# A one-layer transformer kernel in float32: the end part moved into both branches, and its steps reordered

## The reference

```
for w in range(16):                       # for each head of 16
    s = (Q*cpm[w]) @ (K*cpm[w]).T * SCALE # 512x512 for each of 8 sequences
    acc += softmax(s*cos(KERR*s*s)) @ V * iw[w]
x1 = ln(x + (acc/16) @ Wo + bo)
h1, h2 = x1 @ sw1.T + sb1, x1 @ sw2.T + sb2
sh = ln(silu(h1)*h2) * s_ln_g + s_ln_b    # 64 wide
shared = sh @ sw3.T + sb3
xm = x1[rows]                             # 256 chosen rows
scores = sigmoid(xm @ eg_w.T + eg_b); e = argmax(scores + exp_bias)
w_s, w_e = softmax([sigmoid(xm @ sg_w.T + sg_b), scores[e]])
z = ln(silu(xm @ ew1[e].T + eb1[e]) * (xm @ ew2[e].T + eb2[e])) * sel_ln_g + sel_ln_b
shared[rows] = shared[rows]*w_s + (z @ ew3[e].T + eb3[e])*w_e
out = ln(x1 + shared)
```

## Time and profile before

| what | value |
|---|---|
| three runs | 3448.43, 3453.41, 3458.12 us (median 3453.41) |
| the profiled execution, its own time | 3451.96 us |
| its span | 3449.9 us |
| ACT busy | 3334.6 us (97%) |
| DVE busy | 3152.2 us (91%) |
| PE busy | 2711.8 us (79%) |

### The profile page before, as it was taken

The page is one execution under the profiler, slowest core; times in us unless marked ns, Lnnn a source line. Parts: engine busy times, 40 slices in busy tenths (PEclk is TensorE's granted clock), DMA queues, the critical chain, the costliest instruction groups (busy, mean ns, idle before and its releaser), DMA issues.

```text
span 3449.9 us, 47792 instructions
## 1 busy us (share of the span) xinstructions
PE 2711.8 (79%) x20599; PEld 778.2 (23%) x20599; DVE 3152.2 (91%) x2977; ACT 3334.6 (97%) x610; POOL 199.5 (6%) x325
## 2 busy tenths in 40 slices
PE   7887778887778887778887788887888887888763
PEld 2222222222222222222222222222222222222222
DVE  8899899899899899899899999999999999999977
ACT  7999999999999999999999999999999999999971
POOL 0000000000000000000010011110011110011111
PEclk8899999999999999999999999999999899999886
DMA  1000000000000000000000000000000000000010
GB/s 50 1 1 1 1 1 1 1 1 1 1 1 1 1 1 1 1 14 1 1 3 1 4 2 4 2 4 1 2 4 2 4 2 1 4 2 4 2 30 28
DMA packets 20759, 16.10 MB, mean 5 GB/s; under 512 B 4225, under 2 KB 18962, under 8 KB 20306
## 3 DMA queue, kind: packets, MB, share of 16 engines
q1 hardware_dynamic: 19282, 12.34, 1.2%
q10 hardware_dynamic: 1152, 0.53, 0.1%
q0 software_dynamic: 128, 0.26, 0.0%
HBM read 7.76 MB, written 5.37 MB: 4 GB/s over the span
## 4 chain that ended last, share of the span: by engine, by line
ACT 61%; issue 30%; ACTq 4%; DVE 3%; PE 2%; DMA 0%; SPq 0%; POOL 0%; DVEq 0%; POOLq 0%
ACT probs L656 56%; ACT probs L653 4%; ACTq L646 4%; PE psum L1273 1%; DVE m_pad L865 0%; ACTq L650 0%; DVE s_t L877 0%; ACT probs L680 0%; DVE probs L1190 0%; DVE probs L928 0%; DMA iw<-nterference_weights_dram 0%; SPq L468 0%; DVE x_p L743 0%; DVE x_p L735 0%; DVE x_p L739 0%
## 5 line engine op out<-in xcount | busy, mean ns | idle before, releaser
L656 ACT ACTIVATE probs<-s_t 128x8192 f32<-128x8192 f32 x447 | 3101.2, 7090 | 2.2 <-PE psum L1273 2.2
L1273 PE MATMUL psum<-probs,v_pad 128*27 128x512 f32 x15232 | 1992.5, 665 | 602.5 <-ACT probs L656 583.8
L1273 PEld LDWEIGHTS psum<-probs,v_pad 128*27 128x27 f32 x15232 | 485.3, 115 | 2036.1 <-issue 1095.5
L723 DVE SCALAR_TENSOR_TENSOR x_y<-s_t,c_last,x_2k 128x2048 f32<-128x2048 f32 (+1 forms) x160 | 344.1, 2150 | 2.3
L735 DVE SCALAR_TENSOR_TENSOR x_p<-x_p,x_y 128x2048 f32<-128x2048 f32 (+1 forms) x160 | 332.6, 2079 | 4.5
L743 DVE SCALAR_TENSOR_TENSOR x_p<-x_p,x_2k 128x2048 f32<-128x2048 f32 (+1 forms) x160 | 332.1, 2075 | 3.9
L731 DVE SCALAR_TENSOR_TENSOR x_p<-x_y 128x2048 f32<-128x2048 f32 (+1 forms) x160 | 330.9, 2068 | 3.3 <-PE psum L756 3.3
L739 DVE SCALAR_TENSOR_TENSOR x_p<-x_p 128x2048 f32<-128x2048 f32 (+1 forms) x160 | 331.5, 2072 | 2.4
L877 DVE COPY s_t<-psum 128x2048 f32<-128x2048 f32 x128 | 292.2, 2284 | 21.8 <-PE psum L839 21.1
L865 DVE TENSOR_REDUCE m_pad<-psum 128x4 f32<-128x2048 f32 x128 | 292.4, 2286 | 10.8 <-PE psum L802 9.7
L756 PE MATMUL psum<-x_p,v_pad 128*27 128x512 f32 x1152 | 174.5, 620 | 51.9 <-DVE x_p L743 51.4
(11 more groups left out here) (240 smaller groups left out, 1116.0 us busy)
## 6 DMA issues: line engine op xcount, KB each, us to landing
s_t<-in_L_attn_x_dram SPq DMA_DIRECT2D x4, 256.0 KB, 6.9
x_next_dram<-x_p SPq DMA_DIRECT2D x1, 1024.0 KB, 4.5
x_group<-x_next_dram SPq DMA_DIRECT2D x1, 1024.0 KB, 4.9
loop_memory<-in_L_attn_x_dram SPq DMA_DIRECT2D x8, 128.0 KB, 2.2
x_dram<-loop_memory SPq DMA_DIRECT2D x8, 128.0 KB, 1.8
out_dram<-loop_memory SPq DMA_DIRECT2D x8, 128.0 KB, 1.8
x_dram<-probs SPq DMA_DIRECT2D x2, 512.0 KB, 3.3
out_dram<-probs SPq DMA_DIRECT2D x2, 512.0 KB, 3.6
```

Of the source, the lines that this page charges most:

```text
L656: nc.scalar.activation(probs[:, (p + w) % 2, :], s_t[:, p, :], ACT.Exp, scale=scales[(p + w) % 2]).then_inc(s["exp_done"], 1)
L723: nc.vector.scalar_tensor_tensor(out=y, in0=scores, scalar=scale, in1=at, op0=ALU.mult, op1=ALU.subtract) \
L1273: last = nc.tensor.matmul(products_of(u, wg)[L * b:L * b + SLOTS * A, :], v_pad[:, p, b * T + kt, c0:c0 + SLOTS * A], probs[:, (p + w) % 2 ...
```

## The change

- **Both branches.** The end part of PE and DVE is called at the end of each branch (`tail_pe`, `tail_dve`), so no jump lies ahead of it; ACT, POOL and SP keep one copy behind the branches.
- **Prepared in unit 31.** DVE's memsets stand in step 5, the sum x+bo (before on POOL) in step 7, and the turning of the experts' weights (PE) and their copies (before on ACT) in step 8. SP's loop ends one chunk early and the last is written out, so that loads of x and of the experts' weights stand between its parts. The scratch memory is laid out so that what is prepared lies in the first buffer of `s_t`.
- **Chosen rows first.** Their turning, gates and products with all experts stand before stages 6 and 7 of the shared branch on PE; the two branches have norms of their own, and the sums and statistics of stage 7 are woven into the chosen rows' steps (`rest_piece`, `rest_out`). The stores and the scatter stay in their order.
- **Silu.** The biases sb1, sb2 are added by a product of one row (`one_row`) into the bank before stage 4, sigmoid replaces exp, 1+ and reciprocal, and DVE multiplies from PSUM chunk by chunk. The same for the gates. ACT loads the table for Sigmoid and later the one for Exp.
- **Gain and shift.** `sw3_t` is scaled by the norm's gain and `sb3` gets sw3 times its shift at the start of the kernel (`ln_col`), so the two instructions per chunk go.
- The masked experts are summed as a tree of halves, no longer by a reduction.

The core of the diff. At the start, ACT (first piece) and PE:

```diff
-            nc.scalar.activation(sw3_t[:].rearrange("p a n -> p (a n)"), psum[:, 6, P:3 * P], ACT.Copy).then_inc(s["ffw_ready"], 1)
+            nc.scalar.activation(sw3_t[:].rearrange("p a n -> p (a n)"), psum[:, 6, P:3 * P], ACT.Copy).then_inc(s["ffw_copied"], 1)
+            act.wait_ge(s["ffw_shifted"], 1)
+            nc.scalar.activation(weighted[:, 0, :], psum[:, 6, 3 * P:4 * P], ACT.Copy)
+            nc.scalar.activation(sw3_t[:].rearrange("p a n -> p (a n)"), sw3_t[:].rearrange("p a n -> p (a n)"), ACT.Copy,
+                                 scale=ln_col[:, 0:1]).then_inc(s["ffw_ready"], 1)
...
+                    nc.tensor.matmul(psum[:, 6, 3 * P:4 * P], ln_col[:, 1:2].broadcast_to([P, P]), sw3_t[:, 0, :],
+                                     start=True, stop=True).then_inc(s["ffw_shifted"], 1)
             if 4 + T <= step < 4 + 2 * T:
                 kt = step - 4 - T
```

PE's end part:

```diff
+        def tail_pe(pe):
+
+            def chunk_stage(stage, c, ready=None):
+
+                ch, k, t0 = chunk_of(c)
+                ff_pe(pe, stage, ch, k, tail_bank(stage, c), comb[:, t0:t0 + ch.k, :], ready)
...
+            for stage in (1, 2):
+                for c in range(TAIL_CHUNKS):
+                    chunk_stage(stage, c)
+            for c in range(TAIL_CHUNKS):
+                pe.wait_ge(s["residual_done"], c + 1)
+                nc.tensor.matmul(tail_bank(4, c).rearrange("p (k e) -> p k e", e=E), one_row[0:1, :],
+                                 rows[0:1, SB12:SB12 + 1, :].broadcast_to([1, TAIL_TILES, E]), start=True, stop=False)
+            for c in range(TAIL_CHUNKS):
+                chunk_stage(3, c, (s["x1_act"], c - HALF + 1) if c >= HALF else None)
+            for c in range(TAIL_CHUNKS):
+                ch, k, t0 = chunk_of(c)
+                ff_pe(pe, 4, ch, k, tail_bank(4, c), None, (s["tt_act"], c - HALF + 1) if c >= HALF else None, biased=True)
+
+            pe.wait_ge(s["gathered"], 16 * MT)
...
+            pe.wait_ge(s["m_act"], 1)
+            gate_bank = psum[:, 3, MT * E:MT * (E + G)]
+            nc.tensor.matmul(gate_bank.rearrange("p (j g) -> p j g", g=G), one_row[0:1, :],
+                             gate_b[0:1, 0:G].rearrange("p (o g) -> p o g", o=1).broadcast_to([1, MT, G]), start=True, stop=False)
+            for j in range(MT):
+                last = nc.tensor.matmul(gate_bank[:, j * G:(j + 1) * G], moe.tt[:, j, :], gate_t, start=False, stop=(j == MT - 1))
+            last.then_inc(s["m_pe"], 1)
+            for j in range(MT):
+                nc.tensor.matmul(tile_of(psum[:, 2, :], j), moe.tt[:, j, :], sw12_t[:], start=True, stop=True)
+            for i in range(2):
+                for j in range(MT):
+                    pe.wait_ge(s["ff_dve4"], LOOP_CHUNKS + 2 * i + j + 1)
+                    last = nc.tensor.matmul(psum[:, 4 + 2 * i + j, :], moe.tt[:, j, :],
+                                            ew_t[:, i * EC:(i + 1) * EC, :].rearrange("p c d -> p (c d)"), start=True, stop=True)
+            last.then_inc(s["m_pe"], 1)
+
...
+                    pe.wait_ge(s["ff_dve6"], LOOP_CHUNKS + 1)
+                chunk_stage(6, c, (s["u_act"], c - HALF + 1) if c >= HALF else None)
+            pe.wait_ge(s["m_dve"], 1)
+            for c in range(TAIL_CHUNKS):
+                chunk_stage(7, c)
```

DVE's end part:

```diff
+            dve.wait_ge(s["bo_added"], 1)
             for c, (ch, k) in enumerate(chunks):
                 dve.wait_ge(s["ff_pe2"], k + 1)
-                last = nc.vector.tensor_tensor(ch.y, src(2, c), x_bo[:, c * TAIL_TILES:(c + 1) * TAIL_TILES, :], ALU.add)
-            link(last)
-            link(tile_stats(rest, rest.y))
+                nc.vector.tensor_tensor(ch.y, src(2, c), x_bo[:, c * TAIL_TILES:(c + 1) * TAIL_TILES, :], ALU.add) \
+                    .then_inc(s["residual_done"], 1)
+                if c:
+                    dve.wait_ge(s["residual_done"], c)
+                    tile_stats(chunks[c - 1][0], chunks[c - 1][0].y)
+            dve.wait_ge(s["residual_done"], TAIL_CHUNKS)
+            link(tile_stats(chunks[-1][0], chunks[-1][0].y))
...
             for c, (ch, k) in enumerate(chunks):
-                dve.wait_ge(s["ff_pe4"], k + 1)
-                nc.vector.tensor_tensor(ch.h, src(4, c), rows[:, SB12:SB12 + 1, :].broadcast_to([P, ch.k, E]), ALU.add) \
-                    .then_inc(s["ff_dve4"], 1)
...
-            dve.wait_ge(s["ff_exp"], LOOP_CHUNKS + TAIL_CHUNKS)
-            nc.vector.tensor_tensor(rest.u, rest.h[:, :, 0:HID], rest.h[:, :, HID:E], ALU.mult)
-            link(nc.vector.tensor_scalar(rest.e, rest.e, 1.0, None, ALU.add))
-            dve.wait_ge(s["m_pe"], 1)
-            nc.vector.tensor_copy(moe.tt[:, 0:MT, :], two(psum[:, 0, :])).then_inc(s["m_dve"], 1)
-            link(nc.vector.reciprocal(rest.e, rest.e))
-            link(nc.vector.tensor_tensor(rest.u, rest.u, rest.e, ALU.mult))
-            link(tile_stats(rest, rest.u))
+                dve.wait_ge(*((s["x1_act"], c - HALF + 1) if c >= HALF else (s["x1_ready"], k + 1)))
+                last = nc.vector.tensor_tensor(ch.x1b, ch.x1, rows[:, SB3:SB3 + 1, :].broadcast_to([P, ch.k, E]), ALU.add)
+            link(last)
+
+            for c, (ch, k) in enumerate(chunks):
+                dve.wait_ge(s["ff_exp"], k + 1)
+                link(nc.vector.tensor_tensor(ch.u, src(4, c)[:, :, 0:HID], ch.e, ALU.mult))
+                nc.vector.tensor_tensor(ch.u, src(4, c)[:, :, HID:E], ch.u, ALU.mult).then_inc(s["ff_dve4"], 1)
+                if c:
+                    dve.wait_ge(s["ff_dve4"], k)
+                    tile_stats(chunks[c - 1][0], chunks[c - 1][0].u)
+            dve.wait_ge(s["ff_dve4"], LOOP_CHUNKS + TAIL_CHUNKS)
+            link(tile_stats(chunks[-1][0], chunks[-1][0].u))
+            rstd_of(link, rest, HID)
+            shifts(rest)
+            for ch, k in chunks[:HALF]:
+                scaled(ch, ch.u, ch.u).then_inc(s["ff_dve5"], 1)
+
             experts_hidden_dve(dve, link)
...
             link(tile_stats(moe, moe.u))
-            rstd_of(link, tail, HID)
-            shifts(tail)
-            own = tail.part(HALF * TAIL_TILES, GT - HALF * TAIL_TILES + 2 * MT)
-            link(scaled(own, own.u, own.u))
...
-                nc.vector.tensor_tensor(ch.xb, src(7, c), ch.x1b, ALU.add)
+            rstd_of(link, moe, HID, rest_piece, 4)
+            link(scaled(moe, moe.u, moe.u))
+            expert = moe.part(MT, MT)
+            link(nc.vector.tensor_tensor(expert.u, expert.u, wide(rows[:, LN_X:LN_X + 1, 0:HID], HID), ALU.mult))
+            link(nc.vector.tensor_tensor(expert.u, expert.u, wide(rows[:, LN_X:LN_X + 1, HID:E], HID), ALU.add))
+
+            def rest_out():
+
+                rest_piece(6)
+                rest_piece(7)
+                rstd_of(link, rest, E)
+                shifts(rest)
+                for ch, k in chunks[:HALF]:
+                    scaled(ch, ch.xb, ch.y).then_inc(s["y2_ready"], 1)
+
+            experts_down_dve(dve, link, rest_piece, rest_out)
             experts_sum_dve(dve, link)
```

DVE in unit 31, and its call of the end part:

```diff
                         if u + 1 < UNITS:
                             prep_dve(dve, w, u + 1, 1 - p)
+                        elif w == 5:
+                            dve.wait_ge(s["exp_done"], u * WA)
+                            experts_memory_dve()
+                        elif w == 7:
+                            residual_dve(dve)
+                        elif w == EXPERTS_STEP:
+                            experts_weights_dve(dve)
...
                 weigh(UNITS - 1, LAST_TURN_STEPS[WA])
+                tail_dve(dve)
             with dve.Else():
```

316 lines of the change are left out of this document (166 added, 150 removed).

## The result

The changed kernel takes 3427.47 us (median of 4 runs, 3426.22 to 3432.05) against 3450.92 us (median of 4, the three of the table ahead and 3447.97): a ratio of 0.9931 with a 95% interval of 0.9912 to 0.9951, so 0.7% faster. In a second group of runs it took 3427.15 us against 3452.08, ratio 0.9927 (0.9915 to 0.9938).

What follows compares the result with a forecast made beforehand. ScalarE's unbroken exponentials bound the units, then one end-part chain, where the change acts. End part -28.9, start +1.2, jump +1.0 make -26.7 on 3451.96: 3425.3, put at 3426 for the median 1.45 higher; range 3417 to 3437.

Steps and rivals of the forecast that it cites:

- the likeliest case: The forecast itself for the whole kernel: 3426 us, own range 3419 to 3433, chance 61%.
- Start, +1.2: Kernel start: TensorE waits for ScalarE's copy before its first scores and makes one more product, costing 1.2 us.
- Unit 31: Last unit of exponentials: VectorE's 6.0 us of added work fit into 16.5 us free, leaving the unit unchanged.
- Head: First part of the end part: statistics end at 3356.7 instead of 3361.8, ScalarE's half at 3363.4 instead of 3369.6.
- Shared SiLU, "the largest term, 21 us": Shared branch's SiLU on VectorE in the end part: done at 3372.3 instead of 3393.3, 21 us with the earlier start.
- some 13 of it is the two long instructions: Within the shared SiLU: removing the reciprocal of 6.54 and the product of 6.52 us gives some 13 us.
- Chosen rows: Middle of the end part: experts' products end at 3380.0, VectorE waits about 1 us; gain 20.6 by 3403.4.
- From store to the turning products it took 8.2 us: Chosen rows: from the second store of x1 at 3363.4, 8.2 us as before, so turning at 3371.7.
- the sign that I gave for this (under 2 us): Check for the chosen rows: experts' products end before VectorE has waited 2 us.
- The end: Last stretch: two norms stand one behind the other and hide the store; scatter near 3416.5, span ends 4.4 us later.
- The 1.0 us I gave the jump at the end: Jump over the other branch, now after VectorE's last instruction: between 0 and 1.9 us, taken as 1.0.
- The rival in which the jump is only moved (+8.3): VectorE's exit takes 6.5 us, and a second jump at the block's end as much: about 3433 us; chance 13%.

Runs made afterwards that it cites:

- the second profile of after: The changed kernel profiled once more with no edit; last exponential ends at 3339.59 us, first scatter 71.20 us behind the last piece of the attention result.
- undisturbed execution of before: The kernel before profiled once more with no edit; the product of 1024 elements takes 1.22 us, not 6.52, and the scatter comes 94.83 us behind the last piece.

## Why the prediction was right

The forecast was 3426 us, the measurement 3427.47 and 3427.15; the likeliest case occurred. A little of that is luck: 3425.3 and 1.45 make 3426.7, not 3426, and the 1.45 stands for a median of before (3453.41) that a fourth run took down to 3450.92. Its steps, against the second profile of after (my times as distances from my own end of the last piece, 3346.2):

- **Start, +1.2.** Right in kind: scores at 31.28 and 31.52, against 29.97 and 29.46 in the two of before: 1.3 to 2.1 where I had 1.2.
- **Unit 31.** Right: 103.36 us against 103.37. The last exponential was to end within 2 us of 3339; it did at 3339.59, but not at 3342.98 in the first execution, where small waits for TensorE over all units are 5.5 us instead of 2.7.
- **Head.** Statistics forecast at 10.5, measured 10.14; ScalarE's half at 17.2 and 16.85. But of the causes I named, neither carries the 5 us alone: put back one at a time, the jump makes 1.3 us and the preparation 0.65, both within what two executions differ by. In the rows of before VectorE's first sum follows GpSimd's late addition, and ScalarE's scaling follows the chain jump, memsets, loads, turning and copies. That these bind together, and that taking out any one of them frees the rest, is my reading; no run puts them all back. (The 0.86 for a one-row product doesn't come out of "the eight of 5.08", which give 0.64; they took 0.56 each, in the gap, and cost nothing.)
- **Shared SiLU, "the largest term, 21 us".** Its end was right: forecast 26.1, measured 25.96. **This is where the working failed:** the step "some 13 of it is the two long instructions" put the product's 6.52 into the kernel's price, although the prediction says in the same place that it is not the shape's. Only 1.22 is; the other 5.3 belong to the profiled execution. The reciprocal's 6.54 is real (1.75 for each quarter). Up to the last statistics the undisturbed execution of before takes 43.4 us, so the term is 17.4, not 21. Over the end part the difference is 23.6 us (94.83 to 71.20), not the 29 that lie between 99.3 and my 70.3. The absolute time was right all the same, since I built it forward from prices of the new instructions, and took the saving off a profiled time that contained the collision.
- **Chosen rows.** "From store to the turning products it took 8.2 us" came out as 9.46 and 10.27, and the eight products as 5.48 and 5.61 instead of 5.08: VectorE waits 2.96 and 4.80, not 1, and the sign that I gave for this (under 2 us) failed. Part of it is that 8.2 was one execution's: the second of before has 9.15. The eight products add another 0.4. The distance of the two stores is a further candidate (8.28 us with 3.25 between them), and not settled. TensorE's clock after idling holds both my 5.08 and the measured 5.48 above the 3.60 at full clock.
- **The end.** Two norms behind one another: right, worth 7 us. Scatter forecast at 70.3, measured 71.20. The tail behind it is 4.9 us (76.14), before 4.4. The 1.0 us I gave the jump at the end is too much: counted from VectorE's last instruction the span ends as late with the jump put back ahead (5.0) as with it behind (5.0 and 5.2). The rival in which the jump is only moved (+8.3) did not occur. The Trainium skill, "Runtime: NRT & Kernel Launch", section "Instruction fetch mechanics", says that a taken branch to a place outside the fetched blocks stalls until they are loaded. At the old place an idle stretch that fits this is there (6.46 and 6.35 us in the two executions of before), though no row shows a load. No row shows either how long VectorE's jump takes at its new place, since none of its instructions follows.

What the second profiles sum to: 23.6 less in the end part, 1.3 more up to the last exponential, 22.3 us (21.8 from span to span, since the tail is longer); the medians say 23.4 and 24.9. Collided executions among the runs of before may be part of the difference.

Of the 23.6 us two parts are shown by undoing them: the reciprocal (6.0) and the split of the last norm (7.1). Not undone by any run are the chosen rows' new order, the SiLU products from PSUM by chunks, the tree and the folded gain and shift. For the last two the rows show prices only: 2.4 us where the reduction took 3.65, and 0.6 where the gains and shifts took 3.15.

## What to carry to other kernels

Take a second profile before calling one long instruction a cost of the kernel: if the same operation is elsewhere a fifth as long, ask whether it hit something in this execution, and what share of executions that is. A jump, a preparation or a shortened instruction is worth only what sticks out behind the wait beside it; here a jump of 6.5 and a preparation of 6 us made 1.3 and 0.65 when undone one at a time, less than two executions of one kernel differ by. Where a store's way to its reader lies bare, an extra chain of small work in front of it can be cheaper than a joined one.

## What the hardware showed that I had not expected

- VectorE's product of two SBUF operands reads as held rather than slowed: in the first profile of before it was recorded from 3375.89 to 3382.41, GpSimd's four additions from 3376.41 to 3381.32. It ended 1.09 us behind the last of them, almost its own 1.22. The additions kept their price (4.91 against 4.92). The Trainium skill, "SBUF — State Buffer", section "Who interferes with whom", says that the port pair which the two engines share is an exclusive lock, and that the order of issue decides who blocks. The trace agrees on the blocking. It doesn't show who came first: the loser is the one with the earlier record, though GpSimd's gather issue (3375.44 to 3376.38) was under way then, and the product let four instructions of GpSimd pass, not one. That stays open.
- The same the other way round, in the steps of the units of the kernel before:

```profile
3311.66 2.27 DVE L739 SCALAR_TENSOR_TENSOR x_p<-x_p 128x2048 f32<-128x2048 f32 x1
3311.82 2.16 POOL L505 TENSOR_TENSOR loop_memory<-loop_memory 128x2 f32<-128x2 f32 x1 [62.69 <-DVE loop_memory L928]
...
3338.76 0.20 POOL L505 TENSOR_TENSOR loop_memory<-loop_memory 128x2 f32<-128x2 f32 x1 [20.26 <-DVE loop_memory L928]
```

  GpSimd's addition of 128x2 takes 0.20 us where VectorE stands still, and 2.16 where it starts 0.16 us into VectorE's instruction of 2.27; it ends 0.05 us behind that. So a small step of GpSimd's norm can take as long as what VectorE does beside it.
- GpSimd's second gather issue takes 0.94 us, but 1.23 and 1.63 in the two executions (one of before, one of its variant without the additions) in which it began while this product ran; both times it ended 0.8 us behind the product. In a third, where it began 0.13 us ahead of the product, it kept its 0.95. So by these rows the product can hold GpSimd too.
- Eight products of 512 columns: 3.60 us at clock 1.00, 5.48 at 0.65 after 3.5 us of idling. In this kernel a wait of TensorE had a price beyond its length.
- ScalarE's table load is 1.28 us, and its next instruction begins 0.01 us behind it (3397.15 to 3398.44 in the first profile after); both lie in waits here.
